# Keys and values of the second chunk taken in turns, rows of x prepared further apart with two more places, block stores two jobs later

## What is computed

```
h   = layernorm(x)
q   = rope(h @ wq)            # 32 heads of 128
k   = rope(ctx @ wk)          # 8 key heads of 128, each serves 4 query heads
v   = ctx @ wv                # 8 value heads of 128
a   = softmax(q k^T / sqrt(128) + mask) v
x   = x + tanh(g_xattn) * (a @ wo)
n   = layernorm(x)
e   = argmax(n @ route_w^T)   # one of 8 experts, its logit is the weight
x   = x + tanh(g_ffn) * weight * (n @ A_e^T) @ B_e^T
```

## Time and profile before

| | |
|---|---|
| median of three runs | 1138.37 us |
| the profiled execution, its own time | 1137.81 us |
| its span | 1136.0 us |
| PE busy | 1099.9 us, 97% of the span |
| DVE / ACT / POOL busy | 907.7 / 636.4 / 611.4 us |
| moved by DMA | 206.26 MB, 182 GB/s in the mean |

### The profile page before, as it was taken

The page is one execution under the profiler, slowest core; times in us unless marked ns, Lnnn a source line. Parts: engine busy times, 40 slices in busy tenths (PEclk is TensorE's granted clock), DMA queues, the critical chain, the costliest instruction groups (busy, mean ns, idle before and its releaser), DMA issues.

```text
span 1136.0 us, 16986 instructions
## 1 busy us (share of the span) xinstructions
PE 1099.9 (97%) x5616; PEld 917.2 (81%) x5616; DVE 907.7 (80%) x1413; ACT 636.4 (56%) x1106; POOL 611.4 (54%) x513
## 2 busy tenths in 40 slices
PE   7989999989999999999999999999999999999997
PEld 6877788768888888888888778888888888888775
DVE  7974868877887878777878999787878887877877
ACT  6562556566666666666666545455555555555441
POOL 4560378868777877777764434344434434334320
PEclk9999999989999999999999999999999999999999
DMA  7768975476464646464459744453535353542201
GB/s 231 238 213 319 346 232 214 139 269 234 143 230 147 230 142 226 152 204 173 161 205 381 240 136 161 149 182 114 197 125 191 116 181 104 175 137 77 74 1 75
DMA packets 93509, 206.26 MB, mean 182 GB/s; under 512 B 8816, under 2 KB 41712, under 8 KB 87536
## 3 DMA queue, kind: packets, MB, share of 16 engines
q1 hardware_dynamic: 93424, 205.18, 53.4%
HBM read 122.31 MB, written 82.84 MB: 181 GB/s over the span
## 4 chain that ended last, share of the span: by engine, by line
PE 57%; DVE 17%; POOL 10%; issue 9%; ACT 4%; DMA 2%; SPq 1%; DVEq 0%; POOLq 0%; ACTq 0%
PE attn L864 20%; PE proj L805 17%; PE score L822 7%; POOL rot L1624 3%; PE attn L767 3%; POOL wq_s L1599 2%; PE turned L833 2%; PE attn L849 2%; PE attn L851 2%; DVE q_r L1093 1%; PE score L767 1%; DVE q_r L1051 1%; DVE row_sum L1122 1%; DVE wo_s L1046 1%; DVE xB L1040 1%
## 5 line engine op out<-in xcount | busy, mean ns | idle before, releaser
L864 PE MATMUL attn<-wo_s,o_s 128*128 128x512 f32 x1536 | 378.9, 396 | 0.8 <-DVE o_s L1142 0.8
L805 PE MATMUL proj<-xB,wq_s 128*128 128x512 f32 x1344 | 337.7, 395 | 4.0 <-ACT copies L1420 2.2
L864 PEld LDWEIGHTS attn<-wo_s,o_s 128*128 128x128 f32 x1536 | 284.0, 189 | 58.5 <-DVE o_s L1142 1.3
L805 PEld LDWEIGHTS proj<-xB,wq_s 128*128 128x128 f32 x1344 | 253.5, 189 | 58.2 <-ACT copies L1420 2.6
L1624 POOL TENSOR_TENSOR rot<-rot,tab 128x512 f32<-128x512 f32 x112 | 170.8, 1526 | 161.6 <-ACT rot L1399 161.2
L1398 ACT ACTIVATE rot<-q_r 64x512 f32<-64x512 f32 x86 | 54.2, 630 | 144.6 <-DVE q_r L1093 139.9
L822 PEld LDWEIGHTS score<-k_r,q_r 128*128 128x128 f32 x1024 | 123.4, 192 | 13.3 <-DVE q_r L1056 7.6
L822 PE MATMUL score<-k_r,q_r 128*128 128x64 f32 x1024 | 122.7, 273 | 2.9 <-DVE q_r L1056 2.9
L1134 DVE TENSOR_TENSOR p_low<-turned,p_high 64x512 fp32r<-64x512 f32 x128 | 88.0, 688 | 42.6 <-ACT p_high L1436 40.6
L1444 ACT ACTIVATE o_s<-attn 128x512 fp32r<-128x512 f32 x128 | 69.8, 595 | 76.8 <-PE attn L851 76.8
L1056 DVE TENSOR_TENSOR q_r<-q_r,rot 128x512 f32<-128x512 f32 x86 | 89.0, 1035 | 17.1 <-POOL rot L1624 11.8
(11 more groups left out here) (193 smaller groups left out, 1695.7 us busy)
## 6 DMA issues: line engine op xcount, KB each, us to landing
wq_kept<-wq_s SPq DMA_DIRECT2D x16, 1792.0 KB, 6.2
wq_s<-wq_kept SPq DMA_DIRECT2D x16, 1792.0 KB, 8.7
v_kept<-vst SPq DMA_DIRECT2D x64, 256.0 KB, 4.5
v_s<-v_kept SPq DMA_DIRECT2D x128, 128.0 KB, 5.0
wo_kept<-wo_s SPq DMA_DIRECT2D x32, 512.0 KB, 3.7
wo_s<-wo_kept SPq DMA_DIRECT2D x32, 512.0 KB, 5.4
k_kept<-kst SPq DMA_DIRECT2D x32, 256.0 KB, 2.5
wq_raw<-in_wq SPq DMA_DIRECT2D x16, 512.0 KB, 6.1
```

Source lines behind the costliest of these rows:

```text
L805: last = e.matmul(dst[:, :], wq_s[:, b % 2, A, s, kt, :], xB[:, B, mv, kt, :], start=(first and kt == 0 and m == 0), stop=(kt == 1 and m = ...
L864: last = e.matmul(attn[bp][:, :], o_s[:, s, bp, h, :], wo_s[n % WO_SLOTS][:, m, :], start=(h == 0 and i == 0), stop=(h == GROUP - 1 and i ...
```

## The change

Three things change. The keys and values of chunk 1 take turns: job 16 is a key, 17 a value, and so on to job 31. The pairs of x stand at other jobs (8, 11, 14, 18 and 34, 36, 38, 40 instead of 8, 11, 13, 16 and 32, 35, 38, 41), have five places (the two new ones lie in a part of `far_raw` that is free between chunk 2's rows and the first copies of query products), and are fetched at a written list of jobs. The blocks of xB are stored beside jobs 24, 26, ..., 36.

```diff
--- before.py
+++ after.py
@@ -64,7 +64,9 @@
     return [("v", i, part) for part in range(len(V_PARTS))]


-JOBS = [*keys_of(0), *values_of(0), *keys_of(1), *values_of(1), *values_of(2), *values_of(3), *keys_of(3), *keys_of(2)]
+
+BOTH_1 = [job for pair in zip(keys_of(1), values_of(1)) for job in pair]
+JOBS = [*keys_of(0), *values_of(0), *BOTH_1, *values_of(2), *values_of(3), *keys_of(3), *keys_of(2)]
 JOB_NO = {job: n for n, job in enumerate(JOBS)}
 K_NO = {job: n for n, job in enumerate(j for j in JOBS if j[0] == "k")}
 V_NO = {job: n for n, job in enumerate(j for j in JOBS if j[0] == "v")}
@@ -98,12 +100,16 @@


 X_PAIRS = [[("x", half, tt, c) for c in range(CHUNKS)] for half in range(HALVES) for tt in range(CHUNK_TILES)]
-X_BESIDE = {8: 4, 11: 5, 13: 6, 16: 7, 32: 0, 35: 1, 38: 2, 41: 3}
-X_TURN, X_COMBINE, X_SPLIT, X_PLACES = 3, 4, 5, 3
+X_BESIDE = {8: 4, 11: 5, 14: 6, 18: 7, 34: 0, 36: 1, 38: 2, 40: 3}
+
+XB_STORE = (24, 26, 28, 30, 32, 34, 36)
+X_TURN, X_COMBINE, X_SPLIT = 3, 4, 5
 X_ORDER = list(X_BESIDE.values())
 X_NO = {pair: n for n, pair in enumerate(X_ORDER)}

-X_FETCH = [6, 8, 9] + [n + X_SPLIT + 1 for n in list(X_BESIDE)[:-X_PLACES]]
+X_PLACE = [0, 1, 2, 0, 3, 4, 1, 2]
+X_BEFORE = [max([p for p in range(n) if X_PLACE[p] == X_PLACE[n]], default=None) for n in range(len(X_PLACE))]
+X_FETCH = [6, 8, 9, 14, 28, 29, 31, 33]


 RING = [("wo", n) for n in range(HEADS)]
@@ -366,7 +372,7 @@
         table_in, gates_in, routed_in = sem("table_in"), sem("gates_in"), sem("routed_in")
         mask_in = [sem(f"mask_in{c}") for c in range(CHUNKS)]
         acc_in = [sem(f"acc_in{t}") for t in range(HALF_TILES)]
-        x_in = [sem(f"x_in{i}") for i in range(X_PLACES)]
+        x_in = [sem(f"x_in{i}") for i in range(max(X_PLACE) + 1)]
         first_in = [sem(f"first_in{i}") for i in range(len(FIRST))]
         xB_moved = [sem(f"xB_moved{i}") for i in range(BLOCKS)]
         raw_in = [sem(f"raw_in{i}") for i in range(RAW)]
@@ -415,8 +421,10 @@
         def x_place(w):


-            turn = x_number(w) % X_PLACES
-            return x_third[:, w[3], :] if turn == X_PLACES - 1 else x_near[:, CHUNKS * turn + w[3], :]
+            turn = X_PLACE[x_number(w)]
+            if turn < 2:
+                return x_near[:, CHUNKS * turn + w[3], :]
+            return x_third[:, w[3], :] if turn == 2 else far_raw[0][:, CHUNKS * (turn - 3) + w[3], :]

         def x_number(w):
             return X_NO[X_PAIRS.index([w[:3] + (c,) for c in range(CHUNKS)])]
@@ -424,7 +432,7 @@
         def raw_here(w):

             if w[0] == "x":
-                return x_in[x_number(w) % X_PLACES], 16 * CHUNKS * (x_number(w) // X_PLACES + 1)
+                return x_in[X_PLACE[x_number(w)]], 16 * CHUNKS * (1 if X_BEFORE[x_number(w)] is None else 2)
             if w in FIRST_NO:
                 return first_in[FIRST_NO[w]], 16
             return raw_in[RING_NO[w] % RAW], 16 * (RING_NO[w] // RAW + 1)
@@ -520,10 +528,12 @@
                 e.dma_start(raw_place(w), raw_source(w)).then_inc(raw_in[n % RAW], 16)

             def fetch_x(no):
-                if no >= X_PLACES:
-                    e.wait_ge(x_low, 4 * (no - X_PLACES) + 4)
+                if X_BEFORE[no] is not None:
+                    e.wait_ge(x_low, 4 * X_BEFORE[no] + 4)
+                elif X_PLACE[no] >= 3:
+                    e.wait_ge(*lows_made(("ctx", 2, KT - 1)))
                 for w in X_PAIRS[X_ORDER[no]]:
-                    e.dma_start(x_place(w), raw_source(w)).then_inc(x_in[no % X_PLACES], 16)
+                    e.dma_start(x_place(w), raw_source(w)).then_inc(x_in[X_PLACE[no]], 16)

             def fetch_wq_raw(b):
                 if b >= 2:
@@ -663,8 +673,8 @@
                     fetch_raw(RAW + (n - 59) // 2)
                 if n:
                     store_job(JOBS[n - 1])
-                if n in range(22, 22 + 2 * BLOCKS, 2):
-                    store_xB((n - 22) // 2)
+                if n in XB_STORE:
+                    store_xB(XB_STORE.index(n))
                 if n == 40:

                     e.wait_ge(*lows_made(("ctx", 3, KT - 1)))
```

## The result

The changed kernel takes 1135.02 us (median of 7 runs, 1134.11 to 1136.67) against 1139.45 for the kernel before on the same chip: a ratio of 0.9959, 95% interval 0.9947 to 0.9971. It is faster by 4.4 us, where 9.0 were forecast. Its profiled execution took 1134.39 us, 3.42 less than that of before.

The account below looks back on a forecast made before the run. PE, busy 97% of the span, was taken as the bound, so only its standstills could be won: 4.97 + 1.39 + 2.74 = 9.10 us, 9.0 kept, 1138.37 - 9.0 = 1129.4 us. The range for 8 times in 10 was 1125.5 to 1134.0.

Parts of the forecast that it names:

- first two terms: PE's waits for key cosines before job 48: gains of 4.97 and 1.39 us, both counted in full.
- the 4.97: PE's 3.53 us wait from 74.46 us plus 1.44 us of slow clock behind it, forecast to go entirely.
- The 1.39 us: PE's wait from 87.60 to 88.99 us, called the tail of the same backlog and forecast to go entirely.
- the first standstill: PE's wait from 74.46 to 77.99 us for DVE's cosines of a key: 3.53 us, forecast to go.
- the second one: PE's wait from 87.60 to 88.99 us for DVE's cosines of a key: 1.39 us, forecast to go.
- The 2.74 us go: PE's wait at the transposes of x at job 35, 116.32 to 119.06 us: 2.74 us, forecast to go entirely.
- Only jobs 36 on wait for a store made four jobs before: Value stores: earlier waits reach eight jobs back, 21.8 us; from job 36 four jobs, 10.9 us, leaving 8.6 for landing.
- The third standstill stays: Rival: DMA still full, stores land 3 us later, a transpose waits near job 36; gain 6.4 us, 1132.0; chance 0.12.
- DVE's own delay: Second-half x pairs: 6.3 us, just covered by 8.2 of slack; growing past that shared chance 0.12 with slow rounds.
- What is won at 156.04 stays won: From job 48 on: nothing is changed and PE's jobs set off all engines, so the gain by then is kept.
- The rival that had this place: Behind job 48: POOL's stretch doesn't move, PE gives time back at query products; gain under 3, about 1136.5; chance 0.05.
- It is wrong if: PE waits for x normalisation at jobs 37 to 43, waits behind job 48 grow equally, or job 48 starts after 150.

Follow-up runs that it names:

- turns alone: Kernel before with one edit, keys and values of chunk 1 taking turns: 1132.36 us, ratio 0.9939.
- copies first: Changed kernel with ACT's copies of transposed x ahead of its copy of the value job of the same number: 1134.82 us.
- pair at 17: Changed kernel with the fourth x pair beside job 17 instead of 18 and blocks of xB stored beside 23, 25, ..., 35: 1134.96 us.
- small blocks: Changed kernel with each block of xB stored and fetched back in its first eighth only: 1131.28 us.
- x alone: Changed kernel with keys and values of chunk 1 in the old order, keeping its x pairs, places, fetches and block stores: 1143.02 us.
- early fetches: Changed kernel with the last two pairs of x fetched at jobs 20 and 22 instead of 31 and 33: 1131.95 us.
- second half wide: Changed kernel with the second half's x pairs beside jobs 34, 37, 40, 42 instead of 34, 36, 38, 40: 1137.38 us.
- first half as before: Changed kernel with first-half x pairs at 8, 11, 13, 16 and block stores beside 22 to 34, as before: 1135.25 us.
- mix: Changed kernel with x pairs at 8, 11, 14, 17, 33, 36, 39, 41, odd-job block stores 23 to 35, x fetches at 17, 20, 23, 37: 1131.88 us.
- both mends: Changed kernel with fourth x pair at 17, block stores beside 23, 25, ..., 35, last two pairs fetched at 20 and 22: 1131.72 us.

## Why the prediction was wrong

**Bounds, standstills, first two terms: right in size.** All of the 4.97 + 1.39 us went, but for 0.27. For the 4.97 the turns were enough, without the fetch and the later pair that the prediction counted too. The 1.39 us it called the tail of the same backlog; the turns alone show that they aren't, since the first standstill is gone there and the second one stands at 1.51. It is there too with the first half's pairs as before, and gone wherever the turns meet the pairs at 14 and at 17 or 18. How these pairs free it was not traced.

**The step that failed** is "So ACT keeps pace to within 0.1 us, and even if it doesn't, a transpose three jobs behind has 8.2 us in hand. The 2.74 us go." The mechanism, the queue six us behind with every fourth value waiting on it, was on paper. Four things in it were wrong. The first shows in the rate over jobs 24 to 36, which the forecast had at 376 GB/s (us, busy by engine, granted clock, DMA share, GB/s):

```profile
77.18:113.11 35.93, 35.66 (x158) 29.20 (x156) 21.42 (x33) 14.78 (x27) 11.91 (x11) 1.00 0.84 301
```

- The delay of a store was mis-sized: 8.5 us for value 32, measured 19.4 (ready at 103.75, released at 123.11). I let the backlog build up from job 24's start and charged what was left at job 35. The pile starts only when the last lows are made, at 87.87, 10.7 us behind job 23's end (77.18) where I had put it one job (2.7) behind: POOL's combinations stood behind key 22's rotation, ACT's splits behind them. So DMA was not full from job 24 on. From 87.87 to value 32's store the queue had five blocks, four tiles of chunk 3, four keys, four values before it and all four pairs of x: 5.2 + 1.05 + 1.05 + 2.1 + 0.5 + 2.1 = 12.0 MB, at the 381 GB/s measured from 100 to 122 us 31.6 us, to 119.5, and a landing of 2.2 or more: by this estimate 121.7 at the least, against 123.11 measured.
- "Only jobs 36 on wait for a store made four jobs before" was misread: value 35 already waits for the store of value 31, and value 34 for that of value 29, five jobs before. ACT stood 5.69 us before value 34 and 4.78 before value 35.
- The forecast called x fetches "now in the thick of it" a point for a rival, and gave them no price beyond their bytes in the mean over jobs 24 to 35. They are 2.1 of these 12.0 MB; taking half of them out was worth 3 us of time.
- The slack was that of one condition. The transposes of a pair need its normalisation, three jobs back, but also ACT's copies of the pair before, which with pairs two jobs apart stand behind a value only two jobs back, 5.4 us instead of 8.2. Here both were late alike (copies first), so this alone cost nothing yet; in the pair at 17 it was what held PE.

**The rivals.** "The third standstill stays", 1132.0, had the right place and cause. Its price was too low, since the wait was longer than before and here the slow clock came with it: 3.80 + 1.51 us, not 2.74. DVE's own delay, on which I spent the rest of the doubt, was no cause (small blocks).

**Kept to the end?** "What is won at 156.04 stays won" was nearly right for the change: 4.31 us at job 48, 3.42 in the whole execution. From job 48 to the first scores it takes the same 64.3 us as before. The rest is lost behind them, where the stretch to the end is 915.5 to 917.9 us long in the thirteen profiles (915.7 before, 916.6 in the changed kernel); what varies there I didn't trace.

In seven of the experiments something goes back ahead of the first scores: x alone, early fetches, second half wide, first half as before, mix, pair at 17 and both mends. PE's wait at a query product near 207 us is 3.2 to 3.5 us there instead of 1.86. In the early fetches the stretch from job 60 to the first scores is 15.33 us instead of 13.97, so 1.36 us of the 9.3 go back. In all seven, and in none of the other six kernels, DVE's split of a weight just ahead takes 1.76 to 1.78 us instead of 0.68, and overlaps a rotation on POOL from its start or nearly so. Here are the changed kernel and then the early fetches:

```profile
205.88 0.68 DVE L1056 TENSOR_TENSOR wo_s<-raw,wo_s 128x512 fp32r<-128x512 f32 x1
206.25 1.46 POOL L1634 TENSOR_TENSOR rot<-rot,tab 128x512 f32<-128x512 f32 x1 [0.84 <-ACT rot L1409]
...
202.45 1.77 DVE L1056 TENSOR_TENSOR wo_s<-raw,wo_s 128x512 fp32r<-128x512 f32 x1
202.25 1.43 POOL L1634 TENSOR_TENSOR rot<-rot,tab 128x512 f32<-128x512 f32 x1 [0.27 <-ACT rot L1409]
```

After the start of job 60, POOL's rotation begins 4.20 us later in both, but DVE's split 4.40 us later in the early fetches and 3.83 in the changed kernel, and then it takes 1.09 us more. That this makes the 1.36 us is read from the traces; no run varied it alone, and what makes DVE 0.57 us later ahead of it stays open. The rival that had this place priced it at over 6 us.

**The signs named ahead.** Right: no wait for kst before job 24 (0.27 us later on), SP's waits for xB under 10 us (7.8). Wrong: DMA at 301 GB/s over jobs 24 to 36 and not over 350 (it was 381 only from 100 to 122 us), job 48 at 151.73 and not near 147, ACT's waits at 20.3 and not under 8, a wait for x of 3.51 us and not under 1, a clock of 0.98 over 60 to 147 us, POOL's combinations up to 8.5 us apart (128.58 to 137.10). Two of the three conditions under "It is wrong if" came true: the wait at job 39 for the copies and the normalisation of x, and job 48 later than 150.

## What to carry to other kernels

Before a buffered store is called hidden, follow that one store: when its data is ready, every byte that is issued ahead of it from the moment the pile begins, and the latest user of its buffer. A mean rate over the stretch hides this. A change of several parts that wins less than its ledger is worth splitting at once: here one part won 7.0 us and the other gave 2.7 of them back. And a wait on several conditions must be cleared for each: the profile named ACT's copies in the changed kernel, and with these ahead it named DVE's normalisation.

## What the runs showed that I had not expected

The stretch before anything was changed doesn't start alike. Job 16 started between 53.60 and 56.94 us in the profiled executions, though PE's work ahead of it is the same; in the latest one (copies first) the first two key jobs took 6.11 and 4.13 us from start to start, against 4.60 and 2.81 in the changed kernel:

```profile
9.75 2.93 PE L777 MATMUL score<-ctxT,wk_s 128*128 128x512 f32 x6 [0.49 <-DVE ctxT L1056]
12.47 4.29 PE L777 MATMUL turned<-ctxT,wk_s 128*128 128x512 f32 x12
```

The granted clock is listed as 1.00 from 6 to 17 us in both, so the cause is not shown. The difference is about as much as the change under study, so single profiles of two kernels are compared from a common job and not from zero.

A full DMA moves fewer bytes when value stores are a larger part of them. The 290 GB/s at a share of 0.98 are a mean with gaps in it; from 144.5 to 152 us in the kernel before, where the queue issued nothing but value stores and DMA had no gap, it is 347. With the small blocks it is 364 from 100 to 120 us, in the changed kernel 385 (us, busy by engine, granted clock, DMA share, GB/s):

```profile
144.50:152.00 7.50, 7.50 (x39) 6.31 (x38) 5.99 (x10) 4.78 (x9) 4.80 (x7) 1.00 1.13 347
100.00:120.00 20.00, 20.00 (x94) 16.66 (x93) 15.17 (x34) 7.24 (x13) 2.99 (x6) 1.00 1.12 364
100.00:120.00 20.00, 20.00 (x94) 16.64 (x93) 9.16 (x19) 4.77 (x9) 1.10 (x2) 1.00 1.06 385
```
